# A residual stack of four layers on one core: weight products that follow their loads, and work moved between the engines of the opening

## What is computed

```
x = x + L0(x, length, log_dt, C, log_A_real, A_imag, D)      # causal convolution by a 64-state kernel, with a skip D and a length mask
x = x + (x @ W1.T + 2 * routed low-rank part(Wr, A, B))       # top 2 of 8 experts, rank 16
x = x + (x @ W2.T + 0.5 * low-rank part chosen by a label)    # 5 labels, rank 32
# layer 3: an element-wise quantized weight
lora_delta = lora_B @ lora_A * 0.5
cb = codebook / max(abs(codebook));  thresholds = (cb[:-1] + cb[1:]) / 2
normalized = (weight + lora_delta) / scale                    # one scale for 128 columns of a row
quantized = cb[searchsorted(thresholds, normalized)]          # 64 codes; a code may never be hit
w_eff = ((quantized - normalized) + normalized) * scale + lora_delta
x = x + x @ w_eff.T
```

## Time and profile before

| | before |
|---|---|
| median of 3 runs | 1037.75 us (1037.08 to 1039.02) |
| the profiled execution: its time, its span | 1038.91 us, 1037.1 us |
| TensorE, its weight loads | 1001.4 us busy (97%), 799.4 us (77%) |
| VectorE | 846.2 us (82%) |
| ScalarE, GpSimd | 428.3 us (41%), 274.8 us (26%) |
| DMA | 72 GB/s mean |

### The profile page before, as it was taken

How to read it: one execution, slowest core, us unless ns; L and a number is a source line. 1 busy time by engine, 2 the same in 40 slices (tenths; PEclk the granted TensorE clock), 3 DMA queues, 4 the chain that set the end, 5 groups by cost and what they waited for, 6 DMA issues and landing times.

```text
span 1037.1 us, 16623 instructions
## 1 busy us (share of the span) xinstructions
PE 1001.4 (97%) x4855; PEld 799.4 (77%) x4855; DVE 846.2 (82%) x1684; ACT 428.3 (41%) x847; POOL 274.8 (26%) x310
## 2 busy tenths in 40 slices
PE   2999999999999999999999999999999999999996
PEld 1555555988888778888888888888888888888885
DVE  5888888999987488888888888888888888888861
ACT  3211313222275445444454435453454445443531
POOL 2200100273455332223322232223222332223100
PEclk9999999999999999999999999999999999999999
DMA  8701010010202344545444554445454544445311
GB/s 257 169 21 61 21 40 1 1 41 1 41 0 42 62 82 74 91 77 103 83 84 78 101 92 76 86 82 103 78 89 74 104 87 80 82 91 99 57 37 41
DMA packets 316659, 74.97 MB, mean 72 GB/s; under 512 B 292490, under 2 KB 309194, under 8 KB 316626
## 3 DMA queue, kind: packets, MB, share of 16 engines
q1 hardware_dynamic: 316626, 74.56, 36.9%
HBM read 57.61 MB, written 16.91 MB: 72 GB/s over the span
## 4 chain that ended last, share of the span: by engine, by line
PE 92%; DVE 2%; ACT 2%; DMA 1%; issue 1%; SPq 0%; DVEq 0%; ACTq 0%
PE bank L633 33%; PE bank L809 13%; PE bank L760 12%; PE bank L623 10%; PE bank L654 4%; PE bank L603 4%; PE bank L592 4%; PE bank L614 3%; PE bank L660 2%; PE bank L768 2%; PE bank L644 1%; PE bank L719 1%; PE bank L581 1%; PE bank L776 1%; PE bank L714 1%
## 5 line engine op out<-in xcount | busy, mean ns | idle before, releaser
L633 PE MATMUL bank<-Mh,strips_r 128*128 128x512 f32 x1024 | 289.9, 395 | 0.0
L633 PEld LDWEIGHTS bank<-Mh,strips_r 128*128 128x128 f32 x1024 | 190.7, 188 | 41.5
L883 ACT ACTIVATE SK<-ZZ 64x448 f32<-64x448 f32 x128 | 73.9, 577 | 211.4 <-DVE ZZ L1168 209.0
L633 PE MATMUL bank<-Ml,strips_r 128*128 128x512 f32 x512 | 160.6, 395 | 0.0
L475 POOL TENSOR_TENSOR Cl<-QC,Ch 128x256 fp32r<-128x256 f32 x32 | 37.2, 1161 | 454.1 <-ACT Ch L865 454.1
L1168 DVE SCALAR_TENSOR_TENSOR ZZ<-ZZ,coef 128x192 f32<-128x192 f32 (+1 forms) x256 | 120.3, 509 | 10.1 <-DVE ZZ L1159 0.3
L760 PE MATMUL bank<-E,A 128*128 128x512 f32 (+1 forms) x384 | 126.1, 489 | 0.0
L633 PEld LDWEIGHTS bank<-Ml,strips_r 128*128 128x128 f32 x512 | 96.2, 188 | 22.6
L760 PEld LDWEIGHTS bank<-E,A 128*128 128x128 f32 x384 | 63.9, 192 | 61.8 <-issue 61.8
L623 PE MATMUL bank<-Mh,strips_r 128*128 128x296 f32 x512 | 110.4, 299 | 0.3 <-DVE strips_r L1187 0.3
L623 PEld LDWEIGHTS bank<-Mh,strips_r 128*128 128x128 f32 x512 | 85.1, 189 | 5.4 <-issue 5.2
(11 more groups left out here) (277 smaller groups left out, 1687.7 us busy)
## 6 DMA issues: line engine op xcount, KB each, us to landing
X<-in_x SPq DMA_DIRECT2D x256, 64.0 KB, 2.6
XT<-in_x SPq DMA_DIRECT2D x256, 64.0 KB, 2.5
out_x<-O SPq DMA_DIRECT2D x64, 256.0 KB, 3.2
toep<-kpad SPq DMA_DIRECT2D x128, 64.0 KB, 2.1
E<-in_L_cond_W SPq DMA_DIRECT2D x8, 512.0 KB, 7.5
W2s<-in_L_cond_W SPq DMA_DIRECT2D x8, 512.0 KB, 4.3
vq<-in_L_cond_weight SPq DMA_DIRECT2D x8, 512.0 KB, 3.4
LA<-in_L_cond_lora_A SPq DMA_DIRECT2D x8, 80.0 KB, 3.4
```

The costliest lines, as they stand in the source:

```text
L633: pe.matmul(psO[nh][:, :], xs[:, c, :], ms[:, c, nh * BANK:(nh + 1) * BANK], start=(c == 0 and n == 0), stop=False)
L883: act.activation(SK[ri * N:(ri + 1) * N, hh, :].rearrange("p (c b) -> p c b", b=B), ZZ[hh * N:(hh + 1) * N, :, ri, :], ACT.Copy).then_inc( ...
```

## The change

What the diff does, part by part:

- **Loads.** SyncE starts with the codebook, the scales (as 8 long rows, to be transposed on TensorE in a new job `scale`) and then W1's eight blocks, each with its own semaphore. B3 and A3 are loaded once, behind W1. ScalarE issues the first block of W2, the state parameters and the ids.
- **TensorE's list.** It begins with `w2t` 0 and `qt0`, which follows W1's blocks one by one; `qt` is cut in four parts, and the small jobs stand between or inside the blocks; a low-rank part of blocks 0 and 1 comes in block 2. Block 1's transposes now stand behind all of `qt0`. `a3` of quarter 0 stands between the `lap` groups; the later `a3` stand at mt = 3, 5, 7, 8 where they stood at 2, 4, 6, 8.
- **GpSimd** computes the exponential of the state parameters and their angles (33 small instructions) between the diagonals of W1.
- **VectorE.** The low parts of B3 come straight from PSUM; the rest of the state parameters (`nat_rest`) stands behind quarter 0; the pair loop has no wait at its end, only one behind the loop, and each compare waits for the last add but one.
- **`kern`** takes 4 heads in one product (16 products instead of 64), between the first products of `("m", 3, 6)`; ScalarE takes the result in four pieces.

```diff
-        order = [("b3t", 0), ("b3t", 1), ("codesT",)] + deltas(0) + [("w2t", 0, 0), ("w2t", 0, 1)]
-        between = {0: [("codes",)], 1: [("nat4",), ("at", 0), ("at", 1), ("wrt",)], 2: deltas(1), 5: deltas(2), NC - 1: deltas(3)}
-        for kt in range(NC):
+        order = [("w2t", 0, 0), ("w2t", 0, 1), ("scale",), ("qt0", 0), ("codesT",), ("qt0", 1), ("codes",), ("w2t", 1, 0), ("w2t", 1, 1)]
+        order += [("qt", 1, 0), ("b3t", 0), ("b3t", 1), ("qt", 1, 1)] + deltas(0) + [("w2t", 2, 0), ("w2t", 2, 1), ("qt", 1, 2)]
+        order += [("at", 0), ("at", 1), ("wrt",)]
+        between = {2: deltas(1)[:2], 3: deltas(1)[2:], 5: [("nat4",)] + deltas(2)[:2], 6: deltas(2)[2:]}
+        for kt in range(2, NC):
+            order += [("qt", kt, 0), ("qt", kt, 1)]
+            if kt == 2:
+                order += [("qt", 0, 3), ("qt", 1, 3)]
             if kt + 1 < NC:
                 order += [("w2t", kt + 1, 0), ("w2t", kt + 1, 1)]
-            order += [("qt", kt)] + between.get(kt, [])
-        order += [("a3", 0, n) for n in range(4)] + [("lap", mt) for mt in range(MT)]
+            order += between.get(kt, []) + [("qt", kt, 2), ("qt", kt, 3)]
+        order += deltas(3)[:2]
+        for mt in range(MT):
+            order += [("lap", mt)] + ([("a3", 0, mt)] if mt < 4 else [])
+        order += deltas(3)[2:]
         for q in range(QUARTERS):
             for mt in range(MT + 1):
                 order += [("m", q, mt)]
-                if q + 1 < QUARTERS and mt in (2, 4, 6, 8):
-                    order += [("a3", q + 1, mt // 2 - 1)]
-        jobs = [j for j in order if j[0] not in ("qt", "m")]
+                if q + 1 < QUARTERS and mt in (3, 5, 7, 8):
+                    order += [("a3", q + 1, (3, 5, 7, 8).index(mt))]
+        jobs = [j for j in order if j[0] not in ("b3t", "qt0", "qt", "m")]
...
+                sp.dma_start(cb[:, :], bass.AP(codebook.tensor, 0, [[0, P], [1, K_CODES]])).then_inc(ld_codes, 16)
+                sp.dma_start(scale8[:, :], scale_log.rearrange("(t p) g a -> t (p g a)", p=P)).then_inc(ld_scale, 16)
+                for it in range(NC):
+                    sp.dma_start(E1[:, it, 0:L], W1[it * P:(it + 1) * P, :]).then_inc(ld_w1[it], 16)
                 load_w2(1)
+                sp.dma_start(B3n[:, :, :], B3_lora.rearrange("(t p) r -> p t r", p=P)).then_inc(ld_b3, 16)
+                sp.dma_start(A3raw[:, :], A3_lora).then_inc(ld_a3, 16)
+                for t in range(QT_TILES):
+                    load_w3(0, t)
+                def next_w2(ot):
+                    sp.wait_ge(stage_full, jobno[("w2t", ot - 2, 1)] + 1)
+                    load_w2(ot)
+                next_w2(2)
...
+                def madd(out, a, scale, b):
+                    w = out.shape[1]
+                    step(pool.tensor_scalar(nx[:, 6, 0:w], a, scale, None, ALU.mult))
+                    step(pool.tensor_tensor(out, nx[:, 6, 0:w], b, ALU.add))
...
+                e1_diagonal(0)
+                a2_diagonal(0)
+                e1_diagonal(1)
+                pool.wait_ge(e1_ready, 2)
+                pool.wait_ge(a2_ready, 1)
+                pool.wait_ge(ld_kgen, 48)
+                step(pool.tensor_scalar(t[0], logs[:, :], -87.0, 88.0, ALU.max, ALU.min))
+                step(pool.tensor_scalar(t[1], t[0], 1.0 / math.log(2.0), MAGIC, ALU.mult, ALU.add))
+                step(pool.tensor_scalar(t[2], t[1], MAGIC, None, ALU.subtract))
+                e1_diagonal(2)
+                pool.wait_ge(e1_ready, 3)
+                madd(t[3], t[2], -LN2_HI, t[0])
+                madd(t[4], t[2], -LN2_LO, t[3])
+                e1_diagonal(3)
...
+                pool.tensor_tensor(rem_n, rem_n, turn_n, ALU.add).then_inc(nat_rem, 1)
+                pool.wait_ge(nat_rem, 1)
+                a2_diagonal(1)
+                a2_diagonal(2)
...
+                def qt0(part):
+                    if part == 0:
+                        pe.wait_ge(a2_ready, 1)
+                        pe.wait_ge(stage_free, jobno[("w2t", 0, 1)] + 1)
+                    for it in range(part * NC // 2, (part + 1) * NC // 2):
+                        pe.wait_ge(e1_ready, it + 1)
+                        for n in range(2):
+                            last = pe.matmul(bank[2 + n][:, :], A2[:, it, 0:P], E1[:, it, n * BANK:(n + 1) * BANK],
+                                             start=(it == 0), stop=(it == NC - 1))
+                    if part == 1:
+                        last.then_inc(qt_main, 1)
+                def qt(kt, part):
+                    if part == 0:
+                        pe.wait_ge(a2_ready, kt + 1)
+                        pe.wait_ge(stage_free, jobno[("w2t", kt, 1)] + 1)
+                        if kt >= 2:
+                            pe.wait_ge(qt_taken, kt - 1)
+                    elif part == 3:
+                        if kt == 0:
                             pe.wait_ge(e1_ready, NC + 1)
-                        for it in range(NC):
-                            last = pe.matmul(bank[s + n][:, 0:b - a], A2[:, it, kt * P:(kt + 1) * P], E1[:, it, a:b],
-                                             start=(it == 0), stop=(it == NC - 1))
-                    last.then_inc(qt_full, 1)
+                        if kt >= 2:
+                            pe.wait_ge(qt_free, kt - 1)
+                    n = (0, 0, 1, 2)[part]
+                    a, b = ((0, BANK), (BANK, L), (L, EW))[n]
+                    for it in (range(0, NC // 2), range(NC // 2, NC), range(NC), range(NC))[part]:
+                        last = pe.matmul(bank[2 + 3 * (kt % 2) + n][:, 0:b - a], A2[:, it, kt * P:(kt + 1) * P], E1[:, it, a:b],
+                                         start=(it == 0), stop=(it == NC - 1))
+                    if part == 2:
+                        last.then_inc(qt_main, 1)
+                    elif part == 3:
+                        last.then_inc(qt_full, 1)
...
+                        heads = slice(4 * g, 4 * g + 4)
+                        last = pe.matmul(bank[2][:, 16 * g:16 * (g + 1)].rearrange("p (h k) -> p h k", k=PARTS),
+                                         Vt[:, heads, :].rearrange("p h r -> p (h r)"), X1T[:, heads, 0:PARTS], start=True, stop=True)
...
+                        if (q, mt) == (LAST_Q, KERN_IN) and kt < 4:
+                            kern(kt)
...
+                act.dma_start(W2s[:, 0, :], W2[0:P, :]).then_inc(ld_w2[0], 16)
+                act.dma_start(logs[:, 0:1], log_dt.rearrange("(h a) -> h a", a=1)).then_inc(ld_kgen, 16)
+                act.dma_start(logs[:, 1:1 + N], log_A_real).then_inc(ld_kgen, 16)
+                act.dma_start(nat[:, 0, :], A_imag).then_inc(ld_kgen, 16)
+                act.dma_start(c_in[:, :, :], C_ri).then_inc(ld_c, 16)
...
+                        act.activation(B3s[0:R3, g * BANK:(g + 1) * BANK], bank[(4, 7)[g]][0:R3, :], ACT.Copy, scale=0.5).then_inc(b3_hi, 1)
+                        if g == 1:
+                            act.wait_ge(ld_a3, 16)
+                            for rows in (slice(0, R3), slice(R3, 2 * R3)):
+                                act.activation(A3hh[rows, :], A3raw[:, :], ACT.Copy).then_inc(b3_hi, 1)
...
+                            for a in range(4):
+                                rows = slice(a * SPAN, (a + 1) * SPAN)
+                                act.activation(Kt[:, :, a::4], bank[2][rows, 0:4 * H].rearrange("p (g h k) -> p h k g", h=4, k=PARTS)[:, a, :, :],
+                                               ACT.Copy).then_inc(kern_taken, 1)
...
+                    dve.wait_ge(b3_hi, g + 1)
+                    dve.scalar_tensor_tensor(B3s[R3:2 * R3, cols], bank[(4, 7)[g]][0:R3, :], 0.5, B3s[0:R3, cols].bitcast(F32),
+                                             ALU.mult, ALU.subtract).then_inc(b3_lo, 1)
...
-                        if not first:
-                            dve.wait_ge(dve_step, at - 1 + c)
+                        dve.wait_ge(dve_step, at - 1 + c)
...
-                                rise_from(first, done, vf, qf, True)
-                                dve.wait_ge(dve_step, done + per)
+                                rise_from(first, done, vf, qf)
                             else:
                                 with dve.Fori(0, worth // 2) as pair:
                                     for u in range(2):
-                                        rise_from(first + 2 * pair + u, done + (2 * pair + u) * per, vf, qf, u == 0)
-                                    dve.wait_ge(dve_step, done + (2 * pair + 2) * per)
+                                        rise_from(first + 2 * pair + u, done + (2 * pair + u) * per, vf, qf)
+                            dve.wait_ge(dve_step, done + per * worth)
...
+                    if q == 0:
+                        nat_rest()
```

327 lines of the change are left out of this document (175 added, 152 removed).

## The result

| | before | changed |
|---|---|---|
| median of 8 runs each (range), us | 1038.13 (1035.79 to 1042.07) | 1034.51 (1032.91 to 1034.79) |
| ratio, 95% interval | 1 | 0.9958 (0.9942 to 0.9974) |
| profiled execution, its span, us | 1038.9, 1037.1 | 1034.49, 1032.7 |
| mean granted clock of TensorE | 0.995 | 0.991 |

The change makes the kernel 3.6 us faster by the medians, 4.4 by the ratio; 1026.5 was forecast, and 1034.5 lies just outside the range of 1020 to 1034. The last row of the table is the first thing to notice: the changed kernel runs at a lower mean clock.

What follows compares the result with a forecast made beforehand. TensorE was taken as the bound (92% of the chain), with VectorE 3.0 us behind. Gains of 7.3 us up to `chunk_states(0)` and 3.9 in `kern` made 11.2: 1038.9 to 1027.7 profiled, median 1026.5, range 1020 to 1034.

Steps and rivals of the forecast that it cites:

- the start: Opening up to quarter 0: first large product at 10.0, `qt0` ends at 26.8, VectorE starts quarter 0 6.0 us earlier.
- quarter 3: VectorE's quantized weight: quarter 3 ready at 274.8 instead of 277.4, from 6.0 earlier start, 11.4 for `nat_rest`, 8.0 saved waits.
- The pairs' waits: VectorE's 12 waits at the ends of threshold pairs, 8.7 us in all: removing them saves 8.0, bounds 0 and 8.7.
- the tail, 4.7: Quarter 3 to `chunk_states(0)`: VectorE's path of 50.9 us shrinks by 4.7, from ScalarE's second sines and state columns.
- the later counts: At `chunk_states(0)`: TensorE alone 8.9 us earlier, VectorE's chain 2.6 + 4.7 = 7.3; the later engine sets the gain, 7.3.
- `kern`, 3.9: `kern` and its group shrink from 9.4 to 3.5 + 2.1 = 5.6 us, a gain of 3.9, bounds 0.5 and 4.5.
- price of a full transpose: Upper bound on the new `kern`'s 32 records: up to 4.2 us instead of the 2.1 taken.
- so I expect no lower level: The new `kern`'s records, 2.1 us between dense products, should not drop TensorE's clock; it was 0.50 beside the next group before.
- the cases: Chances for the whole kernel against a measurable 2.1 us: faster by more 0.86, within 0.07, slower 0.07.
- TensorE decides: Rival: VectorE's chain is shorter (start at 41.5, all 8.7 saved), so TensorE's 12.8 us count: 1025; chance 0.2.
- GpSimd's 33 small instructions: Rival in the opening: they slow VectorE, `codes` holds TensorE from 27 on, 5 us, 1031.5; chance 0.1.
- `nat_rest` is not paid for: Rival between quarters 0 and 1: its 11.4 us outweigh start and saved waits, 1.8 us slower, 1039.6; chance 0.08.

Runs made afterwards that it cites:

- e1: Changed kernel with the wait at the end of every pair of thresholds put back: 1039.35 us, ratio 1.0021 to the kernel before.
- e3: Changed kernel with `nat_rest` ahead of quarter 0 instead of behind it: 1022.37 us, ratio 0.985 to the kernel before.
- e10: Changed kernel with ten unused products in TensorE's wait for quarter 3, ahead of `a3`(3, 0): 1030.35 us, ratio 0.9934 to the kernel before.
- e15: Changed kernel with ten unused products ahead of `a3`(3, 0) and the diagonal waited for only ahead of `m`(3, 0)'s products 7 and 8: 1030.08 us, ratio 0.9923.
- e6: Changed kernel with A3b's diagonal waited for only ahead of products 7 and 8 of `m`(3, 0): 1028.74 us, ratio 0.9912 to the kernel before.
- e13: Kernel before with the new `kern` alone (16 products of four heads among `m`(3, 6)'s, four copies of Kt): 1036.39 us, ratio 0.9983.
- e4: Kernel before with only the waits at the pairs' ends removed: 1035.54 us, ratio 0.998 to the kernel before.
- e11: Changed kernel with `nat_rest` ahead of quarter 0 and the diagonal waited for only ahead of `m`(3, 0)'s products 7 and 8: 1022.74 us, ratio 0.9858.
- e2: Changed kernel with the old `kern` (64 products of one head, single copy of Kt, behind `chunk_states(0)`): 1034.37 us, ratio 0.9961.

## Why the prediction was wrong

**Right: the start.** First large product at 10.57 (10.0), end of `qt0` 26.8 (26.8, with the 2.5 us charged for the low level; 2.1 are seen), `qt` 1 at 29.65 (30.2). The new wait there, 0.78 us, is the small one forecast. Quarter 0 started at 40.66, 2.8 us earlier than I thought; 1.5 of that is the second spell at the lower level that I had charged and that did not come.

**Right: quarter 3, partly by luck.** 274.28 against 274.8. `nat_rest` takes 11.1 us behind quarter 0 (11.4). The pairs' waits are worth 8.2 (8.0) by e1, 0.5 of it because e1 started quarter 0 later. The 2.8 us of the earlier start do not arrive: the path from quarter 0 on is 233.6 us, 2.3 longer than the sum. The sum had left the durations of VectorE's quantizing instructions as they were. They are busy for 213.7 us, where they were busy for 209.5 before, and for 209.6 in e3. The largest part is in the compares (`step_t`), 64.6 us for 58.1. Two of them fall beside GpSimd's two large subtractions:

```profile
185.10 6.28 DVE L1516 TENSOR_SCALAR step_t<-vq,steps 128x1024 f32<-128x1024 f32 x2
...
187.48 3.35 POOL L594 TENSOR_TENSOR Ml<-LAp,Mh 128x1280 fp32r<-128x1280 f32 x1
```

6.28 us for two, where 1.52 is usual. That GpSimd accounts for all of the 4.2 us is not shown. So two errors cancelled: an earlier start and a slower path.

**Right as a chain, wrong as the sum: the tail, 4.7.** VectorE's part of it came out: its powers are done 34.9 us behind quarter 3, where they took 39.1, and where TensorE did not slow down `chunk_states(0)` came 46.3 (e10), 45.7 (e15) and 45.6 us (e6) behind quarter 3, 46.2 forecast. (Only in e15 does TensorE wait there for VectorE, 0.36 us; in e10 and e6 TensorE's own list took as long.) In the changed kernel itself it came at 49.4. The step that failed is "the later counts": I set TensorE at 275.0 for quarter 3's transposes, "about when VectorE is ready", and let it run at full clock from there. It was there at 269.45, because the first `m` came at 182.90 and not at 188.5. Of these 5.6 us, 1.9 are a spell at the lower level that I had charged and that did not come (the granted clock is 1.00 from 28.90 to 182.90), 0.6 are the start, and 3.1 were charged too much for the transposes, the deltas and the waits between the blocks; the seven blocks, `lap` and `a3` came as charged (110.2 us with the rest of `qt` 0, and 22.2). An engine that is earlier than forecast seemed harmless. But it then waited 4.85 us, ran at the lower level, waited again at `m`(3, 0), where the diagonal came 2.2 us late (0.54 before, and no term of the sum), and again ran at the lower level. TensorE so took the lead back from VectorE with a lateness that its own earliness had caused, 2.7 us at `chunk_states(0)`.

**Wrong in size: `kern`, 3.9.** Two parts. The price of a record: 32 of them add 3.7 us to a group of 3.4 at full clock (e1, e3, e10, e13), 0.115 each, where `wrt`'s 0.066 had been taken for them; the bound "price of a full transpose", 0.13, was the right neighbour. Eight records of each kind take 0.96 (`kern`), 1.04 (transposes of 128x128) and 0.66 us (`wrt`); the first two have weights of 128x128, `wrt` of 8 rows, and whether that is the reason no run tests. This makes 7.1 for 5.6: 1.5 us. And the clock: "so I expect no lower level" held in e1, e3, e10 and e13, but not in the changed kernel, where it cost another 3.3 (10.4). I had read that stretch's clock as a matter of what runs in it; e10 shows that it also depends on what went before: the same `kern` runs at 1.00 if the wait at 269.5 is filled. That the wait alone decides is not shown, for in e1 it was longer and `kern` ran at 1.00 too.

Together, at `kern_transpose`: forecast 327.9 (321.0, 1.3 for `chunk_states`, 5.6), measured 335.38, 7.5 us later; 2.7 of it in the tail, 4.8 in `kern`. `toep`, waited for 0.65 less than before, gives a little back: 4.4 us of gain where 11.2 were forecast. Small slips of the sums play no part: `kern` and its group are 9.5 us in the rows, not 9.4, the path to the end of the deltas adds up to 43.1, not 43.5, TensorE's terms to 188.4, and the cases to 0.85 and 0.08, not 0.86 and 0.07.

**The rivals.** "TensorE decides" did not come true, though both of its conditions did: quarter 0 started before 41.5, and the pairs' waits (8.7) are gone. VectorE was still the later one, because its instructions ran slower, and TensorE had time to spare and lost it. GpSimd's 33 small instructions, 0.24 to 0.70 us each, ended at 28.84 and held nothing by more than 0.8 us. Where GpSimd did slow VectorE was beside quarter 2, in the two rows above. "`nat_rest` is not paid for" did not win, but named the right place: it is the one piece of work whose position decides between 1034.5 and 1022.4, and I priced it at its duration, 11.4 (15.4 on VectorE's path by e3), without asking whether the new start had idle time for it. It had 13.4 us, visible only after the change, but the forecast's own dates (`codes` near 27, B3's copies, deltas to 43.5) contain it.

**What the mean clock explains, and what it doesn't.** Of the kernel before, 29 runs beside e1 to e4 went from 1035.48 us at a mean granted clock of 0.998 to 1041.61 at 0.992: 0.006 of 1037 us is 6.2 us, and 6.1 is the difference. So most of this kernel's scatter goes with the length of its low stretches. The changed kernel's own runs don't follow: from 0.996 to 0.991, 5 us by the same reckoning, they go only from 1032.9 to 1034.6, 1.6 us. A low stretch costs its half only where TensorE would not have waited anyway, and no profile shows the runs at 0.996. What they cost the changed kernel is therefore best read from e10, 4.2 us by the medians and 2.5 by the ratios, and not from the mean.

What stays open: how the low level on `kern` comes to depend on a wait 55 us ahead of it (it was absent in e1 too, with a longer wait there; and some executions of e10, e11 and e15 run at 0.995 to 0.997, 2 to 3 us slower, with no profile of theirs to say where). Whether the second and third stretch follow from what stands ahead of each, or from the first one, is open as well: in e2, with the old `kern`, they began at nearly the same times, and in e10, with the same second wait, neither came.

## What to carry to other kernels

When an engine gets ahead of its supplier, ask what it does in the meantime: a TensorE that waited 5 us here came back at half clock, and ten useless products in the gap made the kernel 2.5 to 4 us faster. A saving on one engine should therefore be given together with the same saving on the one that feeds it, or with work to fill the gap. Price a moved piece of work by the idle time at both places in the new schedule, and by what it shifts beside another engine's work, not by its duration; and place a wait where the operand is read, not at the head of the group (e6).
